# A fused feed-forward kernel with its head in another order: the first products pass by pass, one weight tile in three pieces, four x tiles loaded singly

## The chip, the cores and the metric

The kernel runs on one core of a Trainium2 chip. The metric is device time in microseconds (us) of one execution; the kernel before takes 534.44 us (median of 3 runs, 534.39 to 534.46).

## The reference, cut to what matters

```python
xn = _layernorm(x)                                   # x: 1024 tokens x 512
# first feed-forward block (w1, w3: 1792 x 512; w2: 512 x 1792)
def _binary_diff_weight(w, base):
    d = w - base
    coeff = jnp.mean(jnp.abs(d))                     # ONE number for the whole matrix
    return base + coeff * jnp.sign(d)
W1, W2, W3 = (_binary_diff_weight(...) for the three pairs)
g = silu(einsum(silu(xn @ W1.T) * (xn @ W3.T), W2))
# second block: a 4-bit attention-like linear part and a 4-bit feed-forward part with low-rank terms
s = attn_and_ffn_4bit(xn)
return x + s * g
```

What matters for the change is the coefficient. A weight tile of the gate matrix W1 can't be finished before the mean of |w1 - mean_w1| over all of W1 is known, so 7.3 MB of weights and means have to be in before it. The same holds for W3 ("up") and W2 ("down") later.

## The kernel before, in words

Weights are kept as a high and a low part (fp32r), and a product is made in three passes: high x high, high x low, low x high (`PASSES`). A "chunk" is 128 of the 1792 inner rows; a chunk's weight tile is 128 x 512. Tokens come in two halves of 512 (`th` 0 and 1), so a chunk's gate projection is 2 x 12 matmuls of 128 x 512 columns. The hidden dimension is in four blocks `hc` of 128. x is eight tiles of 128 tokens (`TT`), transposed on the tensor engine.

The head, all in an order written out by hand for each engine:

- SyncE issues all large loads in one queue: x in four DMAs of two tiles each (L473), then the scan tiles (`load_scan`: two chunks of w and two of mean each, 512 KB and 512 KB; five per matrix, numbered 0 to 4 gate, 5 to 9 up, 10 to 14 down) and the units (`load_unit`: the first four chunks of each matrix, 256 KB w and 256 KB mean; 0 to 3 gate, 4 to 7 up, 8 to 11 down) in turn. Five scan slots; a slot is loaded anew only when its signs are taken (`scan_sign`) and its absolute values are summed (`scan_abs`, `scan_abs_dve`).
- VectorE makes the statistics of x (`statistics`, `inverse_root`, `normalise`), the low parts of the transposed x (`x_low`), the differences (`scan_subtract`, L1095; `unit_subtract`, L1106), some sums (`scan_sum`, L1101), the sum over columns (`take_part`, L1147) and the coefficient (`take_coeff`, L1152). Then it makes the weights: unit 1 in two halves (`split_make`, L1165; `split_low`, L1175), units 2 and 3 whole (`unit_make`, `unit_low`).
- ScalarE makes the high parts of x (`x_high`), the signs (`scan_signs`), the rest of the sums (`sum_apart`, `unit_sum`) and the high parts of the weights (`split_high`, L747; `unit_high`, L754).
- GpSimd makes the differences of units 0, 1, 2, 4, 5 and 6, and the low part of unit 0's mean (`early_low`).
- TensorE transposes x (L1663), with filler transposes of the identity in the gaps (`warm`, L1654), and three times over for the last tile (`AGAIN`). Unit 0 is special: its products start before the coefficient is known. `early_mean(th)` (L1677, 12 matmuls) multiplies its mean and `early_signs(th)` (L1688, 8 matmuls) its signs; VectorE puts the two together later (`early_scale`, `early_add`). In the midst of `early_signs(1)` stands `total(GATE)` (L1695), the small matmul that sums the column of partial sums over the partitions. Then `project(1, GATE, 0)` (L1726) waits for the first half of unit 1 (`half_lo`) and goes on through `project(c, GATE, th)` for chunks 1 to 4. The up coefficient's sum, `total(UP)`, stands in the midst of `project(4, GATE, 0)`, after its ninth matmul; `total(DOWN)` stands behind `project(2, UP, 1)`.

After the head come phases for the chunks 4 to 27 and "down" stages between them, with TensorE busy almost without a break.

## Time and profile before

| | |
|---|---|
| median of 3 runs | 534.44 us |
| the profiled execution's own time | 534.48 us |
| span of the profile | 532.7 us |
| TensorE matmul busy | 519.8 us (98%), 2352 matmuls |
| VectorE busy | 443.0 us (83%) |
| ScalarE busy | 328.5 us (62%) |
| GpSimd busy | 94.6 us (18%) |
| DMA | 76.73 MB; the queues full up to about 66 us, mean 144 GB/s over the span |

The span is measured from the first instruction to the last, the time of a run is 1.8 us longer. Times in rows are microseconds from the start of the span. On each engine an instruction starts up to 0.1 us before the end that is recorded for the one ahead of it, so distances between steps are taken from start to start where the engine is dense.

### The profile page before, as it was taken

How to read it: one execution, taken by the hardware profiler on the slowest of the kernel's cores; microseconds unless marked ns; L12 is line 12 of the kernel's file. 1: busy time of each engine (PE TensorE's matmuls, PEld its weight loads, DVE VectorE, ACT ScalarE, POOL GpSimd, SP SyncE). 2: the span in 40 equal slices, each digit the busy share in tenths (PEclk: the TensorE clock that was granted, in tenths of full speed). 3: DMA queues.
4: the chain of work that ended last, by engine and by line, in shares of the span. 5: the costliest groups of instructions: out<-in, count | busy, mean ns of one | idle time of the engine just before them, and what ended most of it. 6: DMA issues, size and time to landing. Idle time of an engine off the chain costs nothing.

```text
span 532.7 us, 6530 instructions
## 1 busy us (share of the span) xinstructions
PE 519.8 (98%) x2352; PEld 432.1 (81%) x2352; DVE 443.0 (83%) x520; ACT 328.5 (62%) x455; POOL 94.6 (18%) x106
## 2 busy tenths in 40 slices
PE   4999999999999999999999999999999999999997
PEld 3778888888888888888888888888888888888886
DVE  6989998988896988865898888999999898874447
ACT  2979978557546655446648557968776585464310
POOL 1311002003100310022003121300310040004491
PEclk9999999999999999999999999999999999999999
DMA  8999905045711491059228994941592387127503
GB/s 337 394 401 404 385 8 168 15 137 98 197 54 46 76 234 49 1 106 223 56 70 160 250 217 90 186 101 40 109 187 47 74 163 144 36 46 161 135 20 139
DMA packets 31745, 76.73 MB, mean 144 GB/s; under 512 B 3873, under 2 KB 7297, under 8 KB 31585
## 3 DMA queue, kind: packets, MB, share of 16 engines
q1 hardware_dynamic: 21632, 57.42, 34.4%
q0 software_dynamic: 9792, 18.88, 20.5%
q8 instruction: 19, 0.31, 0.2%
q14 instruction: 14, 0.11, 0.1%
q10 hardware_dynamic: 288, 0.02, 0.0%
HBM read 53.23 MB, written 2.10 MB: 104 GB/s over the span
## 4 chain that ended last, share of the span: by engine, by line
PE 95%; DVE 3%; DMA 1%; issue 0%; ACT 0%; SPq 0%
PE up_ps L1726 28%; PE gate_pair L1726 27%; PE down_pair L1767 11%; PE up_ps L1767 9%; PE down_ps L1767 7%; PE side_ps L1810 2%; PE down_pair L1726 2%; PE down_pair L1677 1%; PE up_ps L1887 1%; PE gate_pair L1887 1%; PE down_pair L1887 1%; DMA xn<-in_x 1%; PE down_pair L1849 1%; PE gate_pair L1767 1%; PE down_pair L1782 1%; DVE xn L1135 1%
## 5 line engine op out<-in xcount | busy, mean ns | idle before, releaser
L1726 PE MATMUL up_ps<-xT,gu 128*128 128x512 f32 x648 | 151.9, 390 | 0.0
L1726 PE MATMUL gate_pair<-xT,gu 128*128 128x512 f32 x624 | 148.4, 390 | 0.9 <-DVE gu L1175 0.9
L1726 PEld LDWEIGHTS up_ps<-xT,gu 128*128 128x128 f32 x648 | 121.6, 188 | 25.1
L1726 PEld LDWEIGHTS gate_pair<-xT,gu 128*128 128x128 f32 x624 | 117.2, 188 | 25.4 <-DVE gu L1175 1.4
L655 POOL DMA_DIRECT2D y<-y_part x64 | 55.4, 878 | 338.3 <-ACT y_part L819 337.1
L806 ACT ACTIVATE h<-up_ps 128x512 fp32r<-128x512 f32 x52 | 31.1, 597 | 110.1 <-DVE up_ps L1242 57.0
L865 ACT ACTIVATE ramp<-codes,bend_bias 128x1536 f32<-128x1536 uint8 x56 | 88.1, 1580 | 1.9 <-DVE acc L1350 1.6
L1350 DVE SCALAR_TENSOR_TENSOR acc<-ramp,acc 128x1536 f32<-128x1536 f32 x42 | 73.6, 1753 | 4.9 <-ACT ramp L865 4.3
L1767 PE MATMUL down_pair<-h,dn 128*128 128x512 f32 x249 | 60.9, 390 | 0.0
L1767 PEld LDWEIGHTS down_pair<-h,dn 128*128 128x128 f32 x249 | 46.8, 188 | 9.8
L1247 DVE TENSOR_TENSOR h<-up_ps,h 128x512 fp32r<-128x512 f32 x52 | 35.8, 688 | 19.7 <-ACT h L806 19.4
L1767 PE MATMUL up_ps<-h,dn 128*128 128x512 f32 x210 | 51.5, 390 | 0.0
L1767 PEld LDWEIGHTS up_ps<-h,dn 128*128 128x128 f32 x210 | 39.5, 188 | 8.1
L1767 PE MATMUL down_ps<-h,dn 128*128 128x512 f32 x159 | 39.2, 390 | 0.0
L845 ACT ACTIVATE attn_ramp<-attn_codes,bend_bias 128x1024 f32<-128x1024 uint8 x32 | 36.7, 1148 | 0.0
L801 ACT ACTIVATE silu_gate<-gate_pair 128x512 f32<-128x512 f32 x48 | 28.2, 588 | 12.5 <-PE gate_pair L1726 12.3
L1767 PEld LDWEIGHTS down_ps<-h,dn 128*128 128x128 f32 x159 | 29.9, 188 | 6.1
L1303 DVE SCALAR_TENSOR_TENSOR attn_acc<-attn_ramp,attn_acc 128x1024 f32<-128x1024 f32 x24 | 29.2, 1219 | 3.0 <-ACT attn_ramp L845 2.9
L1350 DVE SCALAR_TENSOR_TENSOR acc<-ramp,codes 128x1536 f32<-128x1536 f32 x14 | 24.5, 1753 | 4.4 <-ACT ramp L865 4.4
L1242 DVE SCALAR_TENSOR_TENSOR up_ps<-up_ps,silu_gate 128x512 f32<-128x512 f32 x28 | 19.4, 692 | 9.2 <-PE up_ps L1726 9.2
L1360 DVE SCALAR_TENSOR_TENSOR acc<-acc,scale 128x1536 f32<-128x1536 f32 x14 | 24.6, 1757 | 0.4
L819 ACT ACTIVATE y_part<-up_ps 128x512 f32<-128x512 f32 x23 | 13.8, 602 | 11.7 <-PE up_ps L1767 11.7
(227 smaller groups left out, 647.2 us busy)
## 6 DMA issues: line engine op xcount, KB each, us to landing
y<-y_part POOLq DMA_DIRECT2D x64, 256.0 KB, 5.1
scale<-in_scales SPq DMA_DIRECT2D x28, 384.0 KB, 5.5
scan_w<-in_w SPq DMA_DIRECT2D x15, 512.0 KB, 11.0
base<-in_mean SPq DMA_DIRECT2D x9, 768.0 KB, 4.4
scan_mean<-in_mean SPq DMA_DIRECT2D x9, 512.0 KB, 10.1
silu_gate<-in_mean SPq DMA_DIRECT2D x6, 512.0 KB, 12.4
codes<-in_codes SPq DMA_DIRECT2D x14, 192.0 KB, 6.0
xn<-in_x SPq DMA_DIRECT2D x4, 512.0 KB, 5.0
```

The source lines that it names most:

```text
L655: pool.dma_start((y if g < FFN_GROUPS else y2)[:, hq, sl], y_slot(q), accum_op=ALU.add).then_inc(y_added[q % Y_SLOTS], 16)
L801: nc.scalar.activation(silu_buf(k, th), ps[:, :], ACT.Silu, scale=1.0 if k < B0 else UNIT_STEP).then_inc(silu_done, 1)
L806: nc.scalar.activation(h_part(k, HI, th), up_bank(k, th)[:, :], ACT.Copy).then_inc(h_hi, 1)
L845: nc.scalar.activation(attn_ramp[:, s % 2, :, :], attn_codes[:, a % 2, :, :], ACT.Prelu, bias=bend_bias[:, j:j + 1], scale=slope, alpha=le ...
L865: nc.scalar.activation(ramp[:, s % 2, :], codes[:, k % 2, :], ACT.Prelu, bias=bend_bias[:, j:j + 1], scale=slope, alpha=left).then_inc(nf4 ...
L1242: nc.vector.scalar_tensor_tensor(up_ps[th][:, :], up_ps[th][:, :], UNIT_STEP, silu_buf(k, th), ALU.mult, ALU.mult).then_inc(h_made, 1)
L1247: nc.vector.tensor_tensor(h_part(k, LO, th), up_bank(k, th)[:, :], h_part(k, HI, th).bitcast(f32), ALU.subtract).then_inc(h_lo, 1)
L1303: nc.vector.scalar_tensor_tensor(attn_acc[:, a % 2, :, :], attn_ramp[:, s % 2, :, :], end, attn_codes[:, a % 2, :, :] if j == 0 else attn_ ...
L1350: nc.vector.scalar_tensor_tensor(acc[k % 3][:, :], ramp[:, s % 2, :], end, codes[:, k % 2, :] if j == 0 else acc[k % 3][:, :], ALU.min if ...
L1360: nc.vector.scalar_tensor_tensor(acc[k % 3][:, :], acc[k % 3][:, :], UNIT_START, scale[:, :], ALU.add, ALU.mult).then_inc(nf4_scaled, 1)
L1726: last = nc.tensor.matmul(ps[:, :], w[:, w_part, hc * P:(hc + 1) * P], xT[:, x_part, hc, th * HALF:(th + 1) * HALF], start=(hc == 0 and w_ ...
L1767: last = nc.tensor.matmul(down_bank(g, t)[:, :], dn[:, k % DN_SLOTS, w_part, hq * P:(hq + 1) * P], h_part(k, h_p, th), start=(k == ks[0] a ...
```

## The change

- x: the first four tiles are loaded by a DMA each, the last four in two DMAs of two tiles as before. `statistics(0)` waits for each tile by itself.
- TensorE: the last x tile is transposed once (`AGAIN` is gone), and the filler transposes behind the x tiles (`WARM_LOW`, 16) are gone. The 24 matmuls of unit 0's mean are grouped by pass: high x high and low x high for both halves of the tokens first, then high x low beside the signs. The first group waits for one or two of the `x_low` results (because of the banks) and not for all four or eight. `total(GATE)` stands behind all 40 early matmuls, with 5 filler transposes ahead of it and 8 behind it. `project(1, GATE, 0)` becomes `project_split()`: its 8 matmuls on high weights first, by pieces of 128, 128 and 256 columns, then 4 on low weights.
- The coefficient: `ones` holds 1/(INTER*HID), so `total` gives the coefficient itself. `split_make` reads it from the PSUM bank (`side_ps`) without the copy ahead of it, in three pieces; the copy (`keep_coeff`) and one whole `unit_low(1)` follow.
- ScalarE: `early_high` goes ahead of `scan_signs(0)`, `unit_sum(1)` ahead of `sum_apart(2)`, `scan_signs(2)` from ahead of `sum_apart(3)` to behind the pieces of unit 1, `unit_high(3)` ahead of `scan_signs(5)`.
- VectorE: two `x_low` go ahead of `scan_subtract(1)`, the last two ahead of `scan_subtract(2)`.
- GpSimd: `early_low` waits for the normalised x, not for the second scan tile; `unit_subtract(0)`, (1), (2) and (4) follow with one wait ahead of them.

```diff
+PIECES = [(0, P), (P, 2 * P), (2 * P, HID)]
-AGAIN = 3
-WARM_LOW = {1: 6, 2: 5, 3: 5}
+WARM_TOTAL = [5, 8]
...
-            for n in range(4):
+            for t in range(HC):
+                sp.dma_start(xn[:, t:t + 1, :], x[t // 2, :, t % 2:t % 2 + 1, :]).then_inc(x_first[t], 16)
+            for n in range(2, 4):
                 sp.dma_start(xn[:, 2 * n:2 * n + 2, :], x[n]).then_inc(x_loaded[n], 16)
...
-            nc.gpsimd.memset(ones[:], 1.0).then_inc(const_ready, 1)
+            nc.gpsimd.memset(ones[:], 1.0 / (INTER * HID)).then_inc(const_ready, 1)
...
             def early_low():
                 pool.wait_ge(gu_hi, 1)
-                pool.wait_ge(scan_diff, dve_tiles(1))
+                pool.wait_ge(xn_ready, TT)
...
             early_low()
+            pool.wait_ge(scan_diff, dve_tiles(1))
             unit_subtract(0)
-            pool.wait_ge(xT_lo, 4)
             unit_subtract(1)
-            pool.wait_ge(scan_diff, dve_tiles(2))
             unit_subtract(2)
...
+            early_high()
             scan_signs(0)
-            early_high()
...
+            unit_sum(1)
             sum_apart(2)
-            unit_sum(1)
-            scan_signs(2)
             sum_apart(3)
...
-            split_high(0)
-            split_high(1)
+            for n in range(len(PIECES)):
+                split_high(n)
+            scan_signs(2)
             scan_signs(3)
...
+            unit_high(3)
             scan_signs(5)
-            unit_high(3)
...
-                    dve.wait_ge(x_loaded[t // 2], 16)
+                    dve.wait_ge(x_first[t] if t < HC else x_loaded[t // 2], 16)
...
+            def keep_coeff(m):
+                dve.wait_ge(total_ready, m + 1)
+                nc.vector.tensor_copy(coeff[:, m:m + 1], side_ps[:, m:m + 1]).then_inc(coeff_ready, 1)
...
+            def split_make(n):
+                sl = slice(*PIECES[n])
                 dve.wait_ge(unit_sign, SPLIT_UNIT + 1)
+                dve.wait_ge(total_ready, GATE + 1)
                 nc.vector.scalar_tensor_tensor(unit_base(SPLIT_UNIT)[:, sl], unit_raw(SPLIT_UNIT)[:, sl],
-                                               coeff[:, GATE:GATE + 1], unit_base(SPLIT_UNIT)[:, sl], ALU.mult, ALU.add
-                                               ).then_inc(half_made if half == 0 else unit_made, 1)
+                                               side_ps[:, GATE:GATE + 1], unit_base(SPLIT_UNIT)[:, sl], ALU.mult, ALU.add
+                                               ).then_inc(piece_made if n < 2 else unit_made, 1)
...
             take_part(GATE)
-            take_coeff(GATE)
-            split_make(0)
-            split_make(1)
-            split_low(0)
-            split_low(1)
+            for n in range(len(PIECES)):
+                split_make(n)
+            keep_coeff(GATE)
+            unit_low(SPLIT_UNIT)
+            dve.wait_ge(coeff_ready, 1)
...
+            def early_pass(th, w_part, x_part):
+                if w_part == LO:
+                    pe.wait_ge(gu_lo, 1)
+                elif x_part == LO:
+                    pe.wait_ge(xT_lo, TT // 2 * (th + 1))
+                else:
+                    pe.wait_ge(gu_hi, 1)
+                    pe.wait_ge(xT_lo, th + 1)
+                    pe.wait_ge(xT_hi, TT // 2 * (th + 1))
                 for hc in range(HC):
...
+            def project_split():
+                w = gu_weight(SPLIT_UNIT, GATE)
+                for hc in range(HC):
+                    if hc < 2:
+                        pe.wait_ge(piece_hi, hc + 1)
+                    if hc == HC // 2:
+                        pe.wait_ge(gu_hi, SPLIT_UNIT + 1)
+                    for x_part in (HI, LO):
+                        nc.tensor.matmul(gate_bank(SPLIT_UNIT, 0)[:, :], w[:, HI, hc * P:(hc + 1) * P],
+                                         xT[:, x_part, hc, 0:HALF], start=(hc == 0 and x_part == HI), stop=False)
+                pe.wait_ge(gu_lo, gu_count(SPLIT_UNIT, GATE))
+                for hc in range(HC):
+                    last = nc.tensor.matmul(gate_bank(SPLIT_UNIT, 0)[:, :], w[:, LO, hc * P:(hc + 1) * P],
+                                            xT[:, HI, hc, 0:HALF], start=False, stop=(hc == HC - 1))
+                last.then_inc(gate_done, 1)
...
-            early_mean(0)
+            for th in range(2):
+                early_pass(th, HI, HI)
+                early_pass(th, LO, HI)
+            early_pass(0, HI, LO)
             early_signs(0)
-            early_mean(1)
+            early_pass(1, HI, LO)
             early_signs(1)
-            for c in range(1, FIRST + 1):
+            warm(gate_ps[1], WARM_TOTAL[0])
+            total(GATE)
+            warm(gate_ps[1], WARM_TOTAL[1])
+            project_split()
+            project(SPLIT_UNIT, GATE, 1)
+            for c in range(SPLIT_UNIT + 1, FIRST + 1):
                 project(c, GATE, 0, UP if c == FIRST else None)
                 project(c, GATE, 1)
```

## Rows read from the trace of the kernel before

**Rows 1.** The page: chain that ended last by engine; the costliest gate projections.

```profile
PE 95%; DVE 3%; DMA 1%; issue 0%; ACT 0%; SPq 0%
L1726 PE MATMUL gate_pair<-xT,gu 128*128 128x512 f32 x624 | 148.4, 390 | 0.9 <-DVE gu L1175 0.9
```

**Rows 2.** The chain in order of time: start, us, what; unit 1's second chunk.

```profile
37.13 5.44 PE up_ps L1726 x24
```

**Rows 3.** Timeline, TensorE, 0 to 60 us: start, length, instructions, idle before.

```profile
7.64 1.94 PE L1654 MATMUL side_ps<-ident 128*128 128x128 f32 x8 [7.64 <-DVE moments L1117]
...
12.95 1.12 PE L1663 MATMUL up_ps<-ident,xn 128*128 128x128 f32 x8
...
15.82 1.12 PE L1663 MATMUL gate_pair<-ident,xn 128*128 128x128 f32 x8 [0.98 <-DVE xn L1135]
...
29.05 0.32 PE L1695 MATMUL side_ps<-abs_part,ones 128*128 128x1 f32 x2
...
31.36 5.78 PE L1726 MATMUL gate_pair<-xT,gu 128*128 128x512 f32 x24 [0.95 <-DVE gu L1175]
...
49.89 0.28 PE L1695 MATMUL side_ps<-abs_part,ones 128*128 128x1 f32 x2
```

**Rows 4.** Timeline, VectorE, up to the weights of unit 1.

```profile
4.37 2.71 DVE L1114 BATCH_NORM_STATS2 stats<-xn 128x6 f32<-128x512 f32 x4 [3.37 <-DMA xn<-in_x]
...
26.86 0.69 DVE L1106 TENSOR_TENSOR unit_st<-unit_st 128x512 f32<-128x512 f32 x1
...
28.77 0.16 DVE L1147 TENSOR_REDUCE abs_part<-abs_sums 128x1 f32<-128x9 f32 x1
29.41 0.16 DVE L1152 TENSOR_SCALAR coeff<-side_ps 128x1 f32<-128x1 f32 x1 [0.47 <-PE side_ps L1695]
29.91 0.88 DVE L1165 SCALAR_TENSOR_TENSOR unit_st<-unit_st,coeff 128x256 f32<-128x256 f32 x2 [0.34 <-DVE coeff L1152]
30.87 0.82 DVE L1175 TENSOR_TENSOR gu<-unit_st,gu 128x256 fp32r<-128x256 f32 x2
31.61 0.75 DVE L1505 TENSOR_SCALAR silu_gate<-up_ps,coeff 128x512 f32<-128x512 f32 x1
```

**Rows 5.** Timeline, ScalarE, high parts of units 1 and 2.

```profile
30.43 0.81 ACT L747 ACTIVATE gu<-unit_st 128x256 fp32r<-128x256 f32 x2 [0.88 <-DVE unit_st L1165]
...
33.05 0.63 ACT L754 ACTIVATE gu<-unit_st 128x512 fp32r<-128x512 f32 x1 [0.87 <-DVE unit_st L1159]
```

**Rows 6.** Timeline, SyncE, two issues, each with time to landing; then engines, DMA share, GB/s.

```profile
12.34 1.09 SPq L487 DMA_DIRECT2D scan_w<-in_w  x1
DMA to landing us min/median/max: 13.1/13.1/13.1
...
14.64 0.52 SPq L493 DMA_DIRECT2D unit_st<-in_mean  x1
DMA to landing us min/median/max: 12.2/12.2/12.2
...
20.00:27.00 7.00, 7.00 (x36) 5.82 (x34) 7.00 (x10) 6.69 (x14) 3.50 (x3) 1.00 1.03 400
```

**Rows 7.** Timelines of VectorE and ScalarE on the way to the up coefficient.

```profile
37.03 0.74 DVE L1159 SCALAR_TENSOR_TENSOR unit_st<-unit_st,coeff 128x512 f32<-128x512 f32 x1
...
37.44 1.06 ACT L708 ACTIVATE sign_first<-scan_w 128x1024 int8<-128x1024 f32 x1
...
39.43 0.63 ACT L754 ACTIVATE gu<-unit_st 128x512 fp32r<-128x512 f32 x1
...
43.88 1.06 ACT L708 ACTIVATE sign_rest<-scan_w 128x1024 int8<-128x1024 f32 x1 [0.16 <-DVE scan_w L1095]
...
48.96 0.19 ACT L727 ACTIVATION_READ_ACCUMULATOR junk<-unit_st 128x1 f32 x1
...
49.29 0.16 DVE L1147 TENSOR_REDUCE abs_part<-abs_sums 128x1 f32<-128x9 f32 x1
```

More of the change, by code:

```diff
@@ L337, in block_kernel @@
         x1_ps = [down_ps[0], down_ps[1], gate_ps[0], gate_ps[1], down_ps[2], side_ps, up_ps[0], up_ps[1]]
+        x_first = [sem(f"x_first{t}") for t in range(HC)]
         x_loaded = [sem(f"x_loaded{n}") for n in range(4)]
@@ L1523, in _ @@
                 normalise(t)
+            x_low(0)
+            x_low(1)
             scan_subtract(1)
-            for t in range(4):
+            for t in range(2, TT):
                 x_low(t)
-            x_low(4)
-            x_low(5)
             scan_subtract(2)
-            x_low(6)
-            x_low(7)
             scan_subtract(3)
@@ L1660, in _ @@
                 pe.wait_ge(xn_ready, t + 1)
-                for _ in range(AGAIN if t == TT - 1 else 1):
-                    for c in range(HC):
-                        last = nc.tensor.matmul(x_ps[t][:, c * P:(c + 1) * P], xn[:, t, c * P:(c + 1) * P], ident[:],
-                                                is_transpose=True, start=(c == 0), stop=(c == HC - 1))
+                for c in range(HC):
+                    last = nc.tensor.matmul(x_ps[t][:, c * P:(c + 1) * P], xn[:, t, c * P:(c + 1) * P], ident[:],
+                                            is_transpose=True, start=(c == 0), stop=(c == HC - 1))
                 last.then_inc(xT_tr, 1)
@@ L1667, in _ @@
                     warm(side_ps, WARM[t])
-            for low, count in WARM_LOW.items():
-                pe.wait_ge(xT_lo, low)
-                warm(early_ps[0], count)
-            def early_mean(th):
-                pe.wait_ge(gu_lo, 1)
-                pe.wait_ge(xT_lo, TT // 2 * (th + 1))
-                for hc in range(HC):
-                    for w_part, x_part in PASSES:
-                        nc.tensor.matmul(early_ps[th][:, :], gu_weight(0, GATE)[:, w_part, hc * P:(hc + 1) * P],
-                                         xT[:, x_part, hc, th * HALF:(th + 1) * HALF],
-                                         start=(hc == 0 and w_part == x_part == HI),
-                                         stop=(hc == HC - 1 and w_part == LO))
+            def early_pass(th, w_part, x_part):
[7 more added lines that the diff above has]
+                    pe.wait_ge(xT_hi, TT // 2 * (th + 1))
+                for hc in range(HC):
+                    nc.tensor.matmul(early_ps[th][:, :], gu_weight(0, GATE)[:, w_part, hc * P:(hc + 1) * P],
+                                     xT[:, x_part, hc, th * HALF:(th + 1) * HALF],
+                                     start=(hc == 0 and w_part == x_part == HI), stop=(hc == HC - 1 and x_part == LO))
             def early_signs(th):
@@ L1684, in early_signs @@
                 for hc in range(HC):
-                    if th == 1 and hc == 2:
-                        total(GATE)
                     for x_part in (HI, LO):
```

36 lines of the change are left out of this document (9 added, 27 removed).

## Prediction

> **What bounds the kernel now.** I read the page's chain first: TensorE carries 95% of it, and the largest group of gate projections has 0.9 us of idle time in the whole run, all of it ahead of one instruction [rows 1]. So behind the head TensorE is never short of work, and a microsecond saved or lost in the head goes through to the end as long as each later supplier is early enough. In the chain a chunk's 24 matmuls take 5.44 us, 0.227 us each [rows 2]. Then I read TensorE's timeline for the one stall: it is the wait for unit 1 ahead of L1726, from 30.41 to 31.36 us [rows 3]. VectorE's timeline says what that hangs on: the last gate unit's difference starts at 26.86, its last sum follows, the column sum at 28.77, the total on TensorE at 29.05, the coefficient at 29.41, the halves of unit 1 at 29.91, their low parts at 30.87 [rows 3, 4]. Last I asked what sets 26.86. The mean of unit 3 is issued at 14.64 and lands 12.2 us later, at 26.84, with the DMA engines full (share 1.03, 400 GB/s) [rows 6]. VectorE reaches that subtraction as the data arrive. Two limits meet there: VectorE's work and the load stream.
>
> **x tiles.** The statistics start at 4.37, when 512 KB are in, and take 2.71 for four tiles, with the third waiting a little [rows 4]. Single tiles let the first start earlier, but the last of the four lands no earlier than before, so the four end at most 0.6 us sooner; I take 0.4. Nothing of it reaches the coefficient, because the mean of unit 3 still lands at 26.84: the bytes ahead of it are the same. It may land later: SyncE issues two DMAs more (hidden by the backlog of 12 us), and the first 1 MB now comes in rows of 2 KB, as the units do. From the landing of scan tile 4 (12.34 + 13.1 = 25.44) to that of unit 3 the 512 KB of such rows took 1.40 us; at the 400 GB/s of that stretch they would take 1.31 [rows 6]. So 0.09 per 512 KB, 0.18 for 1 MB; with the rounding of the landings 0 to 0.4. I take 0.15 later.
>
> **The work ahead of the coefficient.** VectorE does the same instructions as before in another order, and ScalarE loses `scan_signs(2)` ahead of its sums (0.95 us). Both are then earlier than the data and wait for unit 3. TensorE's early products start a few us sooner, since the passes on high x need only the first `x_low` results; their 40 matmuls are 9.1 us of work and end near 27.1, with the last `x_low` as the latest supplier. That is ahead of the total at 29.2, so it wins nothing by itself; its use is that no product stands behind the total any more. The third-time transposes and 16 fillers that go away lay in the shadow of this wait: nothing.
>
> **From the coefficient to unit 1.** With the landing 0.15 later the column sum is at 28.92, the total at 29.20, and VectorE sees the coefficient at 29.56. The copy and its semaphore (29.41 to 29.91) are gone from the path: -0.50. A piece of 256 columns goes from VectorE to ScalarE in 0.52 (29.91 to 30.43) and from ScalarE onward in 0.44 (to 30.87) [rows 4, 5]. An element costs about 1 ns on either, so a piece of 128 takes 0.39 and 0.33. The high part is enough for TensorE's first pass: 29.56 + 0.39 + 0.33 = 30.28. The fillers behind the total are eight at 0.12 (eight transposes stand 0.96 apart at 12.95): 29.20 + 0.19 + 0.96 = 30.35. I take 30.35, where 31.36 was: 1.01 sooner. Before, TensorE also lost 0.17 within the split unit (5.78 as printed, in which the last matmul counts with its full 390 ns and not with 227: 5.61, against 5.44) [rows 1 to 3]. Now the third piece is needed 4 matmuls later (31.26; ready about 31.1) and the low part 8 matmuls later (32.17; ready at 31.9), so no stall: 1.18 sooner in all. Reading the scalar operand from PSUM is not in the trace; the nearest row is the copy of it from there (0.16 long, like any one-column instruction), so 0 to 0.1 for each piece, 0 taken. `scan_signs(2)`, put behind the pieces, costs 0.95 on ScalarE and falls into its idle 0.87 ahead of unit 2's high part [rows 5]; without that cover unit 2 would be 1 us late, and TensorE, 1.2 ahead, has about 0.9 of room there. SyncE waits for those signs before it loads scan tile 7: its w goes out near 32.1, six us later than before, with the loads of units 5 and 6 and scan tiles 8 and 9 queued behind it. The backlog (12 us between issue and landing) covers 6 us of that wait, so the stream stays full. Without that cover the up sums would be late by what the engines idled.
>
> **What is late next: the up coefficient.** TensorE reaches the total for the up matrix at 49.89 [rows 3]. The column sum that it needs starts at 49.29, and 0.28 later (28.77 to 29.05) the total may start: 49.57. So the up coefficient was 0.32 us from being a stall. TensorE would now arrive at 49.89 - 1.18 = 48.71. Is the column sum sooner too? It waits for ScalarE's last unit sum, read out at 48.96 + 0.19 = 49.15 [rows 7], and ScalarE is dense from 37.44 on but for the 0.16 ahead of 43.88. VectorE's work from coefficient to `early_scale(0)` was 2.20 (29.41 to 31.61). Now: two pieces at 0.27, then 0.52 to ScalarE, 0.44 back, 0.60 for the whole low part: 2.10. With the landing that is a net +0.05, so unit 3 is made at 37.08. `unit_high(3)`, now ahead of `scan_signs(5)`, waits for it: 0.52 + 0.26 for 512 columns gives 37.86, and `scan_signs(5)` starts at 38.38 instead of 37.44, +0.94. Given back are the 0.52 of `unit_high(3)` behind it (39.43) and the idle ahead of 43.88 (0.16, and 0.1 that dense instructions overlap) [rows 7]. That makes +0.14 to 0.16: last sum read out at 49.29, column sum at 49.43, total at 49.71. TensorE waits there for 1.0 us. **Sum:** 49.71 against 49.89, 0.18 us sooner; 1.18 of gain, 1.00 handed back. The down coefficient, 20 us later, need be only that 0.18 sooner, and no wait for it shows before; the rest of the kernel follows TensorE. From the profiled execution's 534.48 this gives 534.3; that execution lies 0.04 above the median, so 534.3 stands. What 0.15 of later landing costs is 0.10 of it, because TensorE waits for the suppliers in any case.
>
> **Rivals.** (a) The up coefficient isn't the next stall: the whole 1.18 stays, 533.3 (534.44 - 1.18). It needs ScalarE's up sums a microsecond earlier. Against it is that ScalarE is dense on that stretch [rows 7] and none of its instructions there is removed. Partial forms (VectorE and ScalarE each 0.2 to 0.4 sooner) end between 533.9 and 534.3. (b) Slower: the array's clock falls in the new gap. Between 27.1 and 30.35 TensorE does nothing but 13 fillers and the total. In this trace eight transposes took 1.94 us from 7.64 on and 1.12 from 12.95 on, the low and the high of its levels (1.2 and 2.4 GHz) by their ratio, though the granted clock is printed as 1.00 for the whole head; the rise came 5.3 us after the first work. If the clock fell and took as long to return, 5.3 us would run at half rate: 2.6 lost, arrival at the up total 51.4, 1.5 later than before: 536.0. It decides only beyond 1.0 us lost, which the wait for the up coefficient absorbs. Against it: the engine sat idle for 0.98 ahead of 15.82 and the eight transposes behind took 1.12 still [rows 3], and the gap's fillers cut it into pieces of about 1.5 us. (c) The head does what it says but the load stream runs dry behind scan tile 7, or unit 1's chain is 0.3 to 0.5 longer than worked out: both end within 0.5 us of the time before, since the wait at the up total takes them up.
>
> The Trainium skill has a rule that speaks for (b): TensorE: Matmul & The Clock Gate, section Part 4: PE-mode transpose, says that a transpose does not count as busy time for the clock gate as a matmul does. By that rule the 13 fillers would not hold the clock and (b) would be likely. The trace disagrees so far: from 7.64 to 12.95 TensorE did nothing but transposes, and they got fast.
>
> **Chances.** The forecast with its small forms (c) has 0.80, and ends within 0.7 us of the time before. Rival (a) in full has 0.09. Rival (b) has 0.07. Some 0.04 are left for a head that is late elsewhere. Changes under 0.2% (1.07 us) are what a measurement of this kernel can't tell well from none. Faster by more: 0.10; within: 0.82; slower by more: 0.08. The range reaches from (a), 533.2, to 535.2, where half of (b)'s loss would end.
>
> **What would show it.** Right: unit 1's gate projection starts near 30.4, right behind the fillers; the last gate unit's subtraction sits at 26.9 to 27.2 behind an idle VectorE, waiting for its DMA; TensorE has a new idle time of about 1 us at the up total, released by VectorE's column sum, which starts near 49.4. Wrong: the column sum for up at 48.5 or earlier (then (a)); projection matmuls 0.45 us apart after 30 (then (b)); DMA share under 1 between 32 and 40 (then (c)); the gate column sum well before 28.7, which would mean that landing did not bind.

## The result, and the profile after

| | before | after |
|---|---|---|
| median of 7 runs in turn on one chip, us | 534.44 (534.39 to 535.53) | 536.30 (535.95 to 536.69) |
| ratio, 95% interval | | 1.0033 (1.0024 to 1.0043) |
| profiled execution, us; its span | 534.48; 532.7 | 536.68; 534.8 |

The change makes the kernel 1.9 us slower. The forecast was 534.3, with a range up to 535.2: the result lies outside it, on the side that had 0.08. Below, what answers to the rows of before.

TensorE's timeline after; the columns are those of [rows 3]:

```profile
8.94 1.94 PE L1646 MATMUL side_ps<-ident 128*128 128x128 f32 x8 [8.94 <-DVE moments L1118]
...
31.11 0.38 PE L1685 MATMUL side_ps<-abs_part,ones 128*128 128x1 f32 x2 [1.34 <-DVE abs_part L1148]
32.37 2.24 PE L1728 MATMUL gate_pair<-xT,gu 128*128 128x512 f32 x8
34.45 1.08 PE L1732 MATMUL gate_pair<-xT,gu 128*128 128x512 f32 x4
35.37 2.89 PE L1712 MATMUL gate_pair<-xT,gu 128*128 128x512 f32 x12
38.10 5.60 PE L1712 MATMUL up_ps<-xT,gu 128*128 128x512 f32 x24
...
51.60 0.38 PE L1685 MATMUL side_ps<-abs_part,ones 128*128 128x1 f32 x2 [0.42 <-DVE abs_part L1148]
```

Unit 1 starts at 32.37, where it was 31.36 [rows 3] and where 30.35 was forecast. So it is 1.01 later than before, less than the coefficient is late, because the chain from coefficient to products is shorter. The total for the up matrix is at 51.60, 1.71 later than before [rows 3], with a wait of 0.42 ahead of it; at the end the span is 2.1 longer. Half of the loss is thus on TensorE at 32 us, and the other half comes back behind: matched one by one from the end, TensorE's products are 1.13 later than before at 40 us, 1.85 at 60 us, 1.88 at 360 us and 2.02 at 380 us. VectorE's timeline, for [rows 4]:

```profile
3.58 0.69 DVE L1115 BATCH_NORM_STATS2 stats<-xn 128x6 f32<-128x512 f32 x1 [2.59 <-DMA xn<-in_x]
4.79 1.36 DVE L1115 BATCH_NORM_STATS2 stats<-xn 128x6 f32<-128x512 f32 x2 [0.52 <-DMA xn<-in_x]
7.69 0.69 DVE L1115 BATCH_NORM_STATS2 stats<-xn 128x6 f32<-128x512 f32 x1 [1.54 <-DMA xn<-in_x]
...
25.61 3.46 DVE L1096 TENSOR_TENSOR scan_w<-scan_w,silu_gate 128x1024 f32<-128x1024 f32 x2
28.99 0.68 DVE L1107 TENSOR_TENSOR unit_st<-unit_st 128x512 f32<-128x512 f32 x1
...
30.90 0.16 DVE L1148 TENSOR_REDUCE abs_part<-abs_sums 128x1 f32<-128x9 f32 x1
31.62 0.36 DVE L1169 SCALAR_TENSOR_TENSOR unit_st<-unit_st,side_ps 128x128 f32<-128x128 f32 x1 [0.56 <-ACT unit_st L740]
32.14 0.76 DVE L1169 SCALAR_TENSOR_TENSOR unit_st<-unit_st,side_ps 128x128 f32<-128x128 f32 x2 [0.16 <-issue]
```

The first statistics start 0.8 earlier than before, and the fourth 1.3 later than the four were over: they wait for a tile of x until 7.69. The last gate unit's difference is at 28.99, 2.13 later than before, and so is the sum over columns for the gate matrix (30.90; called the column sum below). The DMA rate says why. Stretches of before, then of after (columns: stretch, its length, busy us of TensorE, weight load, VectorE, ScalarE, GpSimd, granted clock, DMA share, GB/s):

```profile
3.00:4.00 1.00, 0.00 (x0) 0.00 (x0) 0.00 (x0) 0.00 (x0) 0.00 (x0) 1.00 1.02 386
4.00:5.00 1.00, 0.00 (x0) 0.00 (x0) 0.63 (x2) 0.00 (x0) 0.00 (x0) 1.00 1.08 400
5.00:6.00 1.00, 0.00 (x0) 0.00 (x0) 0.86 (x3) 0.00 (x0) 0.00 (x0) 1.00 1.01 398
6.00:7.00 1.00, 0.00 (x0) 0.00 (x0) 1.00 (x2) 0.00 (x0) 0.00 (x0) 1.00 0.99 397
```

```profile
3.00:4.00 1.00, 0.00 (x0) 0.00 (x0) 0.42 (x1) 0.00 (x0) 0.00 (x0) 1.00 1.10 363
4.00:5.00 1.00, 0.00 (x0) 0.00 (x0) 0.48 (x2) 0.00 (x0) 0.00 (x0) 1.00 0.90 234
5.00:6.00 1.00, 0.00 (x0) 0.00 (x0) 1.00 (x2) 0.00 (x0) 0.00 (x0) 1.00 0.90 238
6.00:7.00 1.00, 0.00 (x0) 0.00 (x0) 0.14 (x1) 0.00 (x0) 0.00 (x0) 1.00 0.93 334
...
33.00:36.00 3.00, 3.00 (x14) 2.34 (x14) 2.62 (x5) 2.81 (x5) 0.84 (x1) 1.00 0.69 234
```

From 4 to 7 us the DMA engines move 234, 238 and 334 GB/s instead of 400, though the share says that they are at work for nine tenths of it: the packets themselves take longer. This fall is called the dip below. In the packet records of before no packet of these microseconds takes over 0.48 us. In after most 2 KB packets take 0.084, but some take up to 1.4. The bytes that are missing by 7 us, (386+400+398+397) - (363+234+238+334) = 412 KB, are 1.0 us at 400 GB/s. Unit 3's mean, [rows 6] before, lands 1.8 later, at 28.65 instead of 26.84. Its row in after's SyncE timeline, and what the trace says of its landing:

```profile
16.15 0.90 SPq L495 DMA_DIRECT2D unit_st<-in_mean  x1
...
DMA to landing us min/median/max: 11.6/12.1/12.5
```

(12.5 is this one's.) The missing bytes don't explain 1.8 us, since part of them is made up by then. The first 27 us, before and then after:

```profile
0.00:27.00 27.00, 18.18 (x106) 15.94 (x107) 21.96 (x51) 16.89 (x31) 6.53 (x12) 1.00 0.96 366
```

```profile
0.00:27.00 27.00, 16.81 (x86) 13.94 (x87) 20.83 (x49) 14.97 (x27) 7.35 (x12) 1.00 0.94 357
```

9 GB/s over 27 us are 243 KB, 0.6 us at 400 GB/s. The rest is in how unevenly they arrive. The trace records sixteen increments of a load's semaphore, presumably one for each DMA engine, and the load has landed with the last. For the w of scan tile 4 they come between 24.87 and 25.49 before, with the median at 25.14. In after they come between 25.02 and 27.31 with the median at 25.51: taken in order, ten of them are 0.1 to 0.4 later than before, four 0.7 to 0.9, and the last two (27.23 and 27.31) 1.8 to 2.0. The spread is there early (w of scan tile 0: 10.87 to 12.87, before 10.35 to 10.90). So most of the stream is little late, a small part of it 2 us, and every load waits for that part. That it is the engines with the long packets is likely but not shown, since packet records name no engine.

The stretch from 33 to 36 is the second departure: the queue was empty while SyncE waited with scan tile 7, whose w went out at 34.32 (before 26.06; 32.1 forecast).

The other 0.3 of the 2.13 is a clash of GpSimd and VectorE. GpSimd's timeline, before and then after:

```profile
23.37 1.30 POOL L641 TENSOR_TENSOR unit_st<-unit_st 128x512 f32<-128x512 f32 x1 [1.16 <-DVE scan_w L1095]
```

```profile
24.80 2.05 POOL L643 TENSOR_TENSOR unit_st<-unit_st 128x512 f32<-128x512 f32 x1 [1.19 <-DMA unit_st<-in_mean]
```

`unit_subtract(2)` takes 2.05 instead of 1.30, and beside it VectorE's two scan differences take 3.46 where the undisturbed pair takes 2.47 (in a run below). Without that VectorE would have been free at 28.0 and would have waited for the data until 28.65. The 28.0 is itself 1.1 later than before, because the statistics of the first four tiles end at 8.38 and not at 7.08: the late x tile is a second path to nearly the same loss.

### The profile page after: what moved, and what is told of

Its sections match the earlier page's. It is cut to its first block, busy times and chain, and to the rows that moved or that the text cites. A ratio compares the mean times of both kernels' runs of the same rounds, so it can differ in the third digit from the quotient of the medians.

```text
span 534.8 us, 6513 instructions
## 1 busy us (share of the span) xinstructions
PE 519.7 (97%) x2341; PEld 430.5 (80%) x2341; DVE 442.6 (83%) x520; ACT 328.4 (61%) x456; POOL 95.3 (18%) x106
## 4 chain that ended last, share of the span: by engine, by line
PE 89%; DVE 5%; ACT 3%; issue 1%; DMA 1%; SPq 0%; DVEq 0%; ACTq 0%
PE up_ps L1712 27%; PE gate_pair L1712 25%; PE down_pair L1769 11%; PE up_ps L1769 9%; PE down_ps L1769 7%; PE side_ps L1812 2%; DMA xn<-in_x 1%; PE up_ps L1889 1%; PE gate_pair L1889 1%; PE down_pair L1889 1%; PE down_pair L1712 1%; DVE scan_w L1096 1%; PE down_pair L1851 1%; PE gate_pair L1769 1%; PE down_pair L1784 1%
## 5 line engine op out<-in xcount | busy, mean ns | idle before, releaser
L1712 PE MATMUL gate_pair<-xT,gu 128*128 128x512 f32 x612 | 145.6, 390 | 0.0
L1712 PEld LDWEIGHTS gate_pair<-xT,gu 128*128 128x128 f32 x612 | 115.0, 188 | 23.7
L807 ACT ACTIVATE h<-up_ps 128x512 fp32r<-128x512 f32 x52 | 31.1, 597 | 110.6 <-DVE up_ps L1236 57.5
```

Source lines behind the costliest of these rows:

```text
L807: nc.scalar.activation(h_part(k, HI, th), up_bank(k, th)[:, :], ACT.Copy).then_inc(h_hi, 1)
L1712: last = nc.tensor.matmul(ps[:, :], w[:, w_part, hc * P:(hc + 1) * P], xT[:, x_part, hc, th * HALF:(th + 1) * HALF], start=(hc == 0 and w_ ...
```

## The experiments

Two ideas stood at the start. The start of the load stream: the single tiles make it slow. The head: the new order itself makes the coefficient late. All runs were timed beside the kernel before; its median was 534.39 to 534.60. Where a diff is "on e5", the base is the kernel of experiment 5. The file's other edits that follow from it (a semaphore list, the matching wait) are left out.

**1. After, with x in four pair loads (e1).**

```
-            for t in range(HC):
-                sp.dma_start(xn[:, t:t + 1, :], x[t // 2, :, t % 2:t % 2 + 1, :]).then_inc(x_first[t], 16)
-            for n in range(2, 4):
+            for n in range(4):
```

> The changed kernel with its x loads put back to four DMAs of two tiles; all else as changed. Theory D (the single x tiles delay the whole load stream): the data rate no longer falls to 184-300 GB/s between 4 and 6.5 us, x tiles 2 and 3 land at 5.8 and unit 3's mean at about 26.9 instead of 28.65. The gate column sum comes at 28.8 to 29.6 (the later end if GpSimd's difference of unit 2 still keeps VectorE waiting), and the time is 534.0 to 534.9. Rival O (the new order of the head costs it, not the loads): the time stays within 0.3 us of the changed kernel's 536.3.

535.54 us, ratio 1.0020 (1.0010 to 1.0030). The dip is gone (407, 380, 357, 410 GB/s from 3 to 7 us) and the column sum falls to 29.45, as expected; the time doesn't: 0.6 above the range. GpSimd, and then VectorE, of this kernel:

```profile
23.06 2.35 POOL L640 TENSOR_TENSOR unit_st<-unit_st 128x512 f32<-128x512 f32 x1 [0.90 <-DMA unit_st<-in_mean]
34.85 1.29 POOL L640 TENSOR_TENSOR unit_st<-unit_st 128x512 f32<-128x512 f32 x1 [9.44 <-DMA unit_st<-in_mean]
```

```profile
24.17 3.45 DVE L1093 TENSOR_TENSOR scan_w<-scan_w,silu_gate 128x1024 f32<-128x1024 f32 x2
29.45 0.16 DVE L1145 TENSOR_REDUCE abs_part<-abs_sums 128x1 f32<-128x9 f32 x1
35.13 1.56 DVE L1175 TENSOR_TENSOR gu<-unit_st,gu 128x512 fp32r<-128x512 f32 x1
```

The same clash as in after, twice. Neither engine slows to a half: one waits until the other's instruction is over. At 34.85 it is VectorE that waits, 1.56 instead of 0.69, and ScalarE's next silu, and the chain to the up coefficient with it, is 0.87 later. The total for up starts at 51.03, TensorE having waited 1.07 for it.

**2. Before, with the single tiles alone (e2).** The change's x loads, statistics waits and nothing else.

> The kernel before with the first four x tiles loaded singly and waited for singly; nothing else. Theory D: the same fall in the data rate, the fourth tile near 7.7 us, unit 3's mean near 28.6, the gate column sum about 1.8 us later than 28.77, and everything after it as much: 535.9 to 536.5. Rival O: 534.4, as before.

536.76 us, ratio 1.0045 (1.0028 to 1.0062). The old head with single tiles is as slow as after (a little above the range), with the same dip (297, 250, 223, 299 GB/s), packets of up to 2.1 us, the fourth tile's statistics at 7.96 and the gate column sum at 30.72. So the loads alone are enough for the whole loss, and the new order isn't needed for it.

**3. After, each single tile one contiguous 256 KB (e3); 4. after, loads of 64 partitions with rows of 4 KB (e4).**

```
+                tile = x[t // 2].rearrange("p c n -> (p c n)").rearrange("(c p n) -> c p n", c=2, p=P)
+                sp.dma_start(xn[:, t, :], tile[t % 2]).then_inc(x_first[t], 16)
...
+                rows = slice(t % 2 * P // 2, (t % 2 + 1) * P // 2)
+                sp.dma_start(xn[rows, t // 2 * 2:t // 2 * 2 + 2, :], x[t // 2, rows]).then_inc(x_first[t], 16)
```

> The changed kernel, but with the first four x tiles contiguous in HBM (256 KB without gaps), so that their 2 KB rows don't lie at a pitch of 4 KB. If the gaps (half rows of 4 KB) make the slow packets: rate as in e1_pairs and a time of 534.0 to 534.9. If the small size of the rows, or the number of DMAs at the start, makes them: 536 to 536.6, with the same fall in the rate.

> The changed kernel, but the first four x loads are halves by partitions: 64 partitions of two tiles each, 256 KB in rows of 4 KB. As many DMAs of the same size as in the changed kernel, with the row size of the kernel before. If the 2 KB rows make the slow start: 534.0 to 534.9. If the number of DMAs (two more at the start, 256 KB each) makes it: 536 to 536.6.

e3: 535.93 us, ratio 1.0027 (1.0017 to 1.0037). Still a dip (367, 330, 281, then 387 GB/s), column sum 29.92: with the gaps of 2 KB in HBM gone it stays, so they are not the cause, though the time is just under the range expected for that. e4: 537.46 us, ratio 1.0056 (1.0041 to 1.0071); the rate stays at 200 to 262 GB/s until 8 us, about half. Its trace has another pattern than the dip: from 2 to 7 us the median 4 KB packet takes 0.28 to 0.31 us where 0.16 is usual, none takes over 0.63, and the sixteen increments of a load stay within 0.3 us (w of scan tile 0: 12.85 to 13.13). So most likely the loads of 64 partitions are slow in themselves, and e4 says nothing on the row size.

**5. e1 without the clash (e5).** VectorE's last two `x_low` go behind `scan_subtract(2)`, and GpSimd waits for that before `unit_subtract(2)`.

```
             unit_subtract(1)
+            pool.wait_ge(scan_diff, dve_tiles(2))
             unit_subtract(2)
...
-            for t in range(2, TT):
+            for t in range(2, 6):
                 x_low(t)
             scan_subtract(2)
+            x_low(6)
+            x_low(7)
```

> e1_pairs with the places of unit 2's difference put back: VectorE takes its last two x_low behind scan_subtract(2), and GpSimd waits for that difference ahead of unit_subtract(2), so that GpSimd works while VectorE reads PSUM. Theory L (GpSimd and VectorE shut each other out while both read two operands from SBUF): GpSimd's row shrinks from 2.35 to 1.3 us, the pair of scan differences from 3.45 to about 2.5, the gate column sum comes at 28.8 instead of 29.45, and TensorE reaches unit 1 at 30.3. The time falls by 0.3 to 0.7 us from e1_pairs, to 534.8 to 535.2; not by all, since unit 4's difference (pinned by its landing near 34.9) now meets another of VectorE's instructions. Rival (the rows are long for another reason, such as the loads): column sum and time stay as in e1_pairs, 535.5.

534.77 us, ratio 1.0009 (0.9999 to 1.0019). TensorE, and then VectorE:

```profile
29.04 0.38 PE L1685 MATMUL side_ps<-abs_part,ones 128*128 128x1 f32 x2 [0.65 <-DVE abs_part L1146]
30.30 2.23 PE L1728 MATMUL gate_pair<-xT,gu 128*128 128x512 f32 x8
...
49.92 0.38 PE L1685 MATMUL side_ps<-abs_part,ones 128*128 128x1 f32 x2 [0.81 <-DVE abs_part L1146]
```

```profile
24.53 2.47 DVE L1094 TENSOR_TENSOR scan_w<-scan_w,silu_gate 128x1024 f32<-128x1024 f32 x2
...
28.82 0.16 DVE L1146 TENSOR_REDUCE abs_part<-abs_sums 128x1 f32<-128x9 f32 x1
...
49.70 0.16 DVE L1146 TENSOR_REDUCE abs_part<-abs_sums 128x1 f32<-128x9 f32 x1 [0.82 <-ACT junk L726]
```

This is the head as the prediction had it: unit 1 at 30.30 (forecast 30.35), 1.06 sooner than before, and then a wait of 0.81 at the up total, which stands at 49.92 where it stood at 49.89. What the new order wins is handed back there, and the time is that of before to within 0.3 us. So e2 and e5 together part the change in two: the loads alone cost 2.3 us on the old head, and the new order without its clash gives nothing. Taken back one after the other the parts are smaller: in the changed kernel the pair loads win 0.8 us (e1) and parting the two engines another 0.8 (e5), because data that are late hide half of the clash (0.3 in after, 0.63 in e1).

**6. e5 with `scan_signs(2)` back between the sums (e6).** It frees scan tile 7's buffer earlier: its w goes out at 25.49 and not at 32.26.

```
             sum_apart(2)
+            scan_signs(2)
             sum_apart(3)
...
-            scan_signs(2)
             scan_signs(3)
```

> e5_no_clash with scan_signs(2) put back ahead of sum_apart(3), so that SyncE sends scan tile 7's w near 26 instead of 33. Theory H (the dry stretch of the queues between 33 and 38 us is hidden): the data rate stays at 400 GB/s there and the time is that of e5_no_clash within 0.2 us. Rival S (the dry stretch delays the up sums or something behind them): the time falls by 0.3 us or more.

535.05 us, ratio 1.0010 (1.0001 to 1.0019); profiled 534.70, beside e5's 534.89. The stream is full now, and nothing else moves by more than 0.11 us (column sum 28.74, up total 49.81). First e5, then e6:

```profile
33.00:36.00 3.00, 3.00 (x14) 2.47 (x14) 3.00 (x6) 1.98 (x5) 1.51 (x1) 1.00 0.97 345
36.00:39.00 3.00, 3.00 (x15) 2.47 (x14) 3.00 (x4) 2.74 (x5) 0.34 (x1) 1.00 0.99 380
```

```profile
33.00:36.00 3.00, 3.00 (x15) 2.49 (x14) 3.00 (x6) 1.91 (x4) 1.56 (x1) 1.00 1.03 396
36.00:39.00 3.00, 3.00 (x15) 2.49 (x14) 3.00 (x4) 2.74 (x5) 0.24 (x1) 1.00 1.03 405
```

The medians differ by 0.28, more than the 0.2 expected but in e5's favour; both kernels have runs near 534.7 and near 535.4. So the dry stretch of e5 costs nothing that shows.

**7. e5 with ScalarE's last two up sums ahead of its signs (e7); 8. e7 with the unit signs first (e9).**

```
             silu(2, 1)
-            scan_signs(8)
             unit_sum(6)
-            unit_signs(4)
             unit_sum(7)
+            scan_signs(8)
+            unit_signs(4)
             scan_signs(9)
```

> e5_no_clash with ScalarE's unit_sum(6) and unit_sum(7) ahead of scan_signs(8) and unit_signs(4). Theory U (the wait at the up total stands for ScalarE's place in the sums): the up column sum comes 0.8 us sooner, bound by VectorE's own last sum, TensorE's wait at the up total shrinks by as much, and the time is 0.5 to 0.8 below e5_no_clash, 534.1 to 534.5. Rival (what is late behind the up total is set by something else, VectorE's weights of units 4 and 5 for one): the time stays at e5_no_clash's.

> e7_up_sums with ScalarE's unit_signs(4) and (5) ahead of scan_signs(8) and (9), since in e7_up_sums VectorE waits 1.0 us for those signs behind the up coefficient and TensorE then waits for unit 4's weights. Theory U carried on: VectorE's two waits there are gone, TensorE starts the up projections near 52.8 instead of 53.1, and the time is 0.2 to 0.5 below e7_up_sums: 534.0 to 534.3, the best of all so far. Rival (the gain is handed back further on, as the 0.4 of e7_up_sums at 53 us had shrunk to 0.1 by the end): 534.3 to 534.5.

e7: 534.51 us, ratio 1.0002 (0.9993 to 1.0011). The up column sum is at 48.86, 0.84 sooner, and TensorE no longer waits at the total. But the time is only 0.26 below e5, where 0.5 to 0.8 was expected. VectorE now waits, for the signs of units 4 and 5:

```profile
48.86 0.16 DVE L1146 TENSOR_REDUCE abs_part<-abs_sums 128x1 f32<-128x9 f32 x1
...
49.96 0.75 DVE L1160 SCALAR_TENSOR_TENSOR unit_st<-unit_st,coeff 128x512 f32<-128x512 f32 x1 [0.31 <-ACT unit_st L738]
51.36 0.75 DVE L1160 SCALAR_TENSOR_TENSOR unit_st<-unit_st,coeff 128x512 f32<-128x512 f32 x1 [0.65 <-ACT unit_st L738]
```

e9 takes these waits away and gives 534.42 us, ratio 1.0001 (0.9992 to 1.0010): the up projections behind that coefficient start at 53.13 (e7 53.11, e5 53.68). Of the 0.8 us won against before at the up total (49.09 and 49.89), 0.4 are left at those projections (before 53.53), 0.3 at 69.58 (before 69.86) and 0.2 in the span (532.5). That is what its rival said: the head's gain is given back by steps. None of these versions beats before.

**9. After again (e8).**

> The changed kernel once more, for a second look at its start. Theory D: some 536.3 again, with a fall in the data rate between 3 and 7 us, though not of the same depth, since the runs of this kernel lie 0.7 us apart and those of the kernel before 0.1 to 0.6. The fourth x tile lands later than 6.2. Rival (the fall was chance): rate at 390 or above from 4 us on, fourth tile at 6.0.

536.12 us, ratio 1.0031 (1.0020 to 1.0043), with the dip (302, 281, 363, 389 GB/s), packets of up to 1.7 us and the column sum at 30.19: the dip is not an accident of one execution, though its depth varies.

**10. e5 with pair loads in rows of 2 KB (e10).** x lies in HBM so that each half of a 512 KB load is contiguous, as short as the singles' rows.

```
-                sp.dma_start(xn[:, 2 * n:2 * n + 2, :], x[n]).then_inc(x_loaded[n], 16)
+                tiles = x[n].rearrange("p c n -> (p c n)").rearrange("(c p n) -> p c n", c=2, p=P)
+                sp.dma_start(xn[:, 2 * n:2 * n + 2, :], tiles).then_inc(x_loaded[n], 16)
```

> e5_no_clash with x tile by tile in HBM, so that its four loads of two tiles each are as many and as large as there, but move rows of 2 KB. Rival R (rows of 2 KB make the slow start): the data rate falls below 350 between 3 and 7 us as in the changed kernel, and the time is 535.8 to 536.4. Theory N (six DMAs, four of them of 256 KB, where four of 512 KB stood, make it): the rate is at 370 or above from 3 us on, the gate column sum comes at 28.8 to 29.0, and the time is 534.7 to 535.0.

535.31 us, ratio 1.0013 (1.0004 to 1.0023); 390, 381, 387, 387 GB/s from 3 to 7 us, no packet over 0.18 us there, column sum at 29.04, 0.22 later than e5's. The time lies between the two expectations. Short rows make no dip. Their price is at most those 0.2 us for 2 MB: at 8 us this kernel is 189 KB behind e5, but 139 KB of that are missing at 4 us already, because its stream begins later.

**11. e5 with singles issued by two engines (e11).** SyncE issues tiles 0 and 2, ScalarE 1 and 3.

> e5_no_clash with the first four x tiles loaded singly, tiles 0 and 2 by SyncE and tiles 1 and 3 by ScalarE ahead of its two small loads. Theory Q (one queue's issues of 256 KB each 0.45 us keep too little in flight at the start): with two queues the rate is at 370 or above from 3 us on, the gate column sum comes at 28.7 to 29.0 and the time is 534.6 to 535.0. Rival Z (single tiles at the start harm whichever queue sends them): a fall below 330 between 3 and 7 us, the gate column sum at 29.5 or later, the time 535.4 or above.

535.91 us, ratio 1.0025 (1.0016 to 1.0035), but in two groups, 534.8 and 535.7 to 536.8. The profile caught one of the first (534.81), with the column sum at 28.78. Its rate is between the two expectations (326, 340, 410, 400 GB/s from 3 to 7 us), no packet there takes over 0.41 us, and the sixteen increments for the w of scan tile 4 lie within 0.43 us. So a somewhat lower rate at the start, without stragglers, costs nothing. On the cause the run is inconclusive: of the slow group there is no trace.

**12. e5 with only tiles 0 and 1 single (e12); 13. e5 with tiles 0 and 1 a pair, 2 and 3 single (e15).**

```
-            for n in range(4):
+            for t in range(2):
+                sp.dma_start(xn[:, t:t + 1, :], x[0, :, t:t + 1, :]).then_inc(x_first[t], 16)
+            for n in range(1, 4):
```

> e5_no_clash with the first two x tiles loaded singly and the other six in three pairs, all by SyncE. If each single load at the start adds to the harm: a smaller fall in the rate than in the changed kernel (280 to 350 in one microsecond between 3 and 6), the gate column sum at 29.0 to 29.8, the time 535.0 to 535.7. If only the third and fourth single do harm (the queue runs thin behind two of them): as e5_no_clash, 534.7 to 534.9.

> e5_no_clash with tiles 0 and 1 as a pair, tiles 2 and 3 singly, then two pairs: e12_one_pair with the singles in the second place. If single loads harm wherever they stand in the first microseconds: as e12_one_pair, 535.4 to 536.4. If only a single load at the head of the queue does: as e5_no_clash, 534.7 to 534.9.

e12: 536.25 us, ratio 1.0029 (1.0016 to 1.0041). That is outside both expectations; the column sum is at 30.56. Two singles do the harm of four. The packets that take up to 1.5 us are 4 KB ones of the pair behind them:

```profile
3.77 1.47 DVE L1116 BATCH_NORM_STATS2 stats<-xn 128x6 f32<-128x512 f32 x2 [2.78 <-DMA xn<-in_x]
7.55 1.29 DVE L1116 BATCH_NORM_STATS2 stats<-xn 128x6 f32<-128x512 f32 x2 [2.31 <-DMA xn<-in_x]
```

So it is not a property of the small loads, nor of their rows. e15: 535.24 us, ratio 1.0012 (1.0002 to 1.0021), a dip of 311, 228, 269 GB/s and the column sum at 29.49, between the two expectations: singles as second and third load harm about half as much.

**14. e5 with an unused 8 KB load behind each of the first three pairs (e13).** What e12 leaves is how fast requests come: a load is issued each 0.45 us, so singles bring 256 KB per 0.45 us (about 570 GB/s), little more than the engines take, where pairs bring twice that. Here the loads are pairs, but brought in at 512 KB per 0.93 us.

```
                 sp.dma_start(xn[:, 2 * n:2 * n + 2, :], x[n]).then_inc(x_loaded[n], 16)
+                if n < 3:
+                    sp.dma_start(y_part[:, n, 0:HEAD], x[0, :, 0, 0:HEAD]).then_inc(spare, 16)
```

> e5_no_clash with its four x loads of 512 KB, but a load of 8 KB (not used) issued behind each of the first three, so that SyncE hands over 512 KB each 0.93 us: as many bytes per microsecond as with single tiles, with pair sizes and 4 KB rows. Theory Q (thin supply at the start makes the slow packets): a fall below 350 between 3 and 7 us, single packets near 1 us, the gate column sum at 29.4 or later, the time 535.4 to 536.4. Rival Z (the single tile's size or form makes them): 370 or above from 3 us on, the gate column sum at 28.8 to 29.0, the time 534.7 to 535.0.

536.05 us, ratio 1.0027 (1.0018 to 1.0037). The windows of this kernel:

```profile
3.00:4.00 1.00, 0.00 (x0) 0.00 (x0) 0.00 (x0) 0.00 (x0) 0.00 (x0) 1.00 1.11 337
4.00:5.00 1.00, 0.00 (x0) 0.00 (x0) 0.58 (x1) 0.00 (x0) 0.00 (x0) 1.00 0.97 348
5.00:6.00 1.00, 0.00 (x0) 0.00 (x0) 0.71 (x2) 0.00 (x0) 0.00 (x0) 1.00 1.05 303
6.00:7.00 1.00, 0.00 (x0) 0.00 (x0) 0.00 (x0) 0.00 (x0) 0.00 (x0) 1.00 0.94 310
```

The dip is there with pairs of 4 KB rows, and packets of 1.06 and 0.97 us. The column sum is at 30.07. The three extra loads are 24 KB, 0.06 us at 400 GB/s; as 384 packets of 64 bytes, each 0.011 us long in the records, they are 0.26 us on each of 16 engines. At least 1.0 of the 1.28 against e5 comes with the slower supply. This run alone can't exclude that the small packets make the dip; e12 has it without them.

**15. e5 with x in two loads of 1 MB (e14).** The other end of that scale.

```
-            for n in range(4):
-                sp.dma_start(xn[:, 2 * n:2 * n + 2, :], x[n]).then_inc(x_loaded[n], 16)
+            for n in range(2):
+                sp.dma_start(xn[:, HC * n:HC * n + HC, :].rearrange("p (m c) d -> p m c d", m=2),
+                             x[2 * n:2 * n + 2].rearrange("m p c d -> p m c d")).then_inc(x_loaded[n], 16)
```

> e5_no_clash with x in two loads of 1 MB, the fullest supply at the start. VectorE can begin only when four tiles are in, near 5.9 us, so its own work is 1.3 us late and the gate column sum comes near 30.0 and the time at 535.8 to 536.1 whatever the loads do. Told apart by the landing of unit 3's mean: theory Q: at 26.7 to 27.0, with a rate of 390 or above from 3 us on and no packet above 600 ns between 3 and 7 us. If larger loads also disturb the start: later than 27.3.

535.94 us, ratio 1.0024 (1.0015 to 1.0033), and the narrowest of all kernels: ten runs within 0.22 us. There is no dip (424, 411, 397, 381 GB/s), and unit 3's mean lands at 14.72 + 11.9 = 26.62, before VectorE needs it. VectorE's own work is late:

```profile
5.83 2.47 DVE L1114 BATCH_NORM_STATS2 stats<-xn 128x6 f32<-128x512 f32 x4 [4.84 <-DMA xn<-in_x]
...
28.43 0.68 DVE L1106 TENSOR_TENSOR unit_st<-unit_st 128x512 f32<-128x512 f32 x1
...
30.33 0.16 DVE L1147 TENSOR_REDUCE abs_part<-abs_sums 128x1 f32<-128x9 f32 x1
```

The statistics start 1.5 us later, and VectorE is dense from 16.76 to 30.33. So the head stands between two walls: loads too small thin the stream, loads too large starve VectorE, and the 512 KB of before lie where both are met.

## Why the prediction was wrong

**What bounds the kernel** was right. A loss in the head goes through to the end. That 2.13 at the column sum and 2.1 of span are alike is chance: the shorter chain takes 1.12 off (1.01 late at unit 1), and the split unit (0.12), the up total (0.58) and later products (0.3) add 1.0 again.

**x tiles: this step failed.** It said 0.15 later, 0 to 0.4, "the bytes ahead of it are the same". They were, but the landing of unit 3's mean came 1.8 later. The term that was mis-sized is this lateness of the landing, 0.15 forecast and 1.8 measured. The bound was taken from a stretch in which the queue was 12 us deep [rows 6]; the loads that the change touches are the first of the queue, where it isn't, and no row of before shows a thin queue there. That the rate depends on how far the requests run ahead was not among the causes bounded at all. The runs show it: singles alone (e2), two singles with pairs behind (e12), and pairs brought in at the singles' pace (e13) all have the dip and a column sum 1.2 to 2.0 later than their base; short rows at the pace of pairs (e10) have none. Nor was it asked whether all of a load comes equally late; its last part decides (25.51 for the median increment of scan tile 4, 27.31 for the last). The "0.4 sooner" for the statistics became 0.8 sooner for the first tile, a wait of 1.54 before the last, and an end 1.3 later than before. That is no small matter either, since VectorE has no slack up to the column sum: in e12 and e13 the second half's statistics start 1.74 and 1.23 later than in e5 (11.36 and 10.85 against 9.62), and the column sum comes 1.74 and 1.25 later.

**The work ahead of the coefficient** was half right. TensorE's products end at 29.2, not at 27.1, still 1.9 ahead of the total. "Both are then earlier than the data" left GpSimd out. With its waits for `xT_lo` and `scan_diff` gone, `unit_subtract(2)` starts beside VectorE's scan differences, which costs 0.3 in after and, with the data on time, 0.63 (29.45 in e1, 28.82 in e5). Both engines work there on operands in SBUF. The Trainium skill, SBUF — State Buffer, section SBUF: two separate sides, says that a VectorE instruction with two SBUF inputs and a GpSimd instruction that reads SBUF exclude each other for the whole instruction. The traces agree: 2.35 against 1.30 on GpSimd, 1.56 against 0.69 on VectorE. `x_low`, which has PSUM for one input, stands beside the same GpSimd work in e5 without a loss on either side (1.30 on GpSimd, 0.68 each on VectorE). That rule spoke against the removed waits, and it wasn't used.

**From the coefficient to unit 1** was right in the main. From column sum to unit 1 took 2.59 before [rows 3, 4] and takes 1.47 in after (30.90 to 32.37) and 1.48 in e5; 1.43 was worked out (28.92 to 30.35). Within it two terms were off: VectorE starts 0.51 behind the total's start instead of 0.36, and the second piece 0.52 behind the first instead of 0.27. Together with a total that starts 0.22 and not 0.28 behind the column sum they add 0.05. The first piece and the fillers are ready together, as worked out (in e5 the piece's high part ends at 30.25, the last filler starts at 30.08). The split unit takes 5.73 (32.37 to 38.10), where no stall was forecast and 5.61 stood before [rows 2, 3]: the 0.17 that it was to win became 0.12 lost.

**scan tile 7 and the backlog** was wrong and harmless. The w goes out at 32.26 in e5 (32.1 forecast), and 2 us later in after, as the head is. "The stream stays full" didn't hold in either: 345 GB/s from 33 to 36 in e5, 234 in after. The 12 us from issue to landing were counted as reserve for a wait of 7.6 (24.68 to 32.26 in e5) and didn't cover it. e6 shows that the dry stretch costs nothing in e5; in after it wasn't tested alone.

**The up coefficient** was right. e5, whose head is as forecast, hands back 0.8 (1.00 forecast) and has its total at 49.92 (49.71 forecast); it ends at 534.77. So even with the loads right the forecast's 534.3 was 0.5 too low, 0.2 of it at this total; the rest stands on TensorE as 0.11 more by 60 us and 0.16 between 360 and 380 us, for reasons that aren't traced, and e5's interval (0.1 below to 1.0 above before) doesn't exclude it. e7 and e9 show that the wall was not the last one.

**The rivals.** (a) didn't occur. (b), the falling clock, didn't either: after the gap from 29.8 to 31.1 the first products are 0.23 to 0.34 apart, as they are before (0.22 to 0.34), and then 0.227, never 0.45, with the granted clock at 1.00; it had the right sign and the wrong mechanism. (c) named the dry stream, but at the wrong place, and held it below 0.5. The row that it asked for (DMA share under 1 between 32 and 40) is there, and the loss isn't from it. The slower case that happened, the stream's start, had no price, only a share in the 0.04 left over.

## What to carry to other kernels

A load cut in two is not free because its bytes are the same: ask how deep the queue is at that point, and take bounds only from a stretch with the same depth; at the start of a kernel, where nothing is queued, loads of 512 KB issued 0.45 us apart kept the engines near 400 GB/s and half of that did not. A rate isn't enough to judge it by: a load lands with its last part, and two late increments of sixteen held up a stream whose median was 0.4 late. When a wait is removed, look at what it kept apart: here it held GpSimd off VectorE. And a gain at the head is worth what the next waits leave of it: measure each wall behind it before the work for the first.

## What the runs showed of the hardware

- **A thin start of the queue.** With 256 KB per 0.45 us or 512 KB per 0.93 us from the first request on, the longest packets between 3 and 8 us take 1.0 to 2.1 us instead of 0.08 (2 KB) or 0.16 (4 KB), and the 16 engines together fall to 220 to 350 GB/s for two to four microseconds; at 512 KB per 0.45 us no packet there takes over 0.55, and the rate is 357 to 410. The stragglers stay: the sixteen increments for the w of scan tile 4 spread over 2.3 us in after, 2.2 in e2, 1.8 in e12, 1.2 in e13, but over 0.3 to 0.6 in before, e5, e10 and e14. Long packets stand again at 36 to 39 us in kernels whose queue had run dry at 33 to 36: up to 0.8 to 1.2 us in after, e7, e12, e13 and e15, but only 0.43 in e5 and 0.50 in e11. Where it hadn't run dry, the longest there is 0.17 (before, e6) and 0.22 (e2). "Thin" names the pattern and not a cause: by 4 us SyncE has issued 2.6 MB in after and 0.76 MB have moved (before 3.7 and 0.76), so there is always something asked for. What makes a packet long is not shown: the trace has no more than its duration. ScalarE's two small loads, in 64-byte rows, are issued at the same time in every kernel but e11, and no run leaves them out. e11's two groups and the varying depth of the dip (the column sum 1.4 to 2.1 later for one and the same pattern, in e8, e2 and after) are open with it.
- **64 partitions, about half the rate:** 205 to 262 GB/s in e4 from 3 to 8 us, with 4 KB packets about twice as long as usual (0.28 to 0.31 in the median until 7 us) and none over 0.57. No run has them with a full supply.
- **Rows of 2 KB against 4 KB:** 381 to 390 against 380 to 410 GB/s, at most 0.2 us for 2 MB (e10, e5).
